# A fused two-layer attention block: VectorE normalises the second half of an attention result before it rounds the last quarter of the MLP's inner values

## What is computed

```
# layer 0
ln = layernorm(x);            x = x + attention(q(ln), k(ln), v(ln), causal) @ w_ao + b_ao     # stage A
ln = layernorm(x);            x = x + attention(q(ln), k(ctx), v(ctx), cross) @ w_co + b_co    # stage B
ln = layernorm(x);            x = x + gelu(ln @ w1 + b1) @ w2 + b2                             # stage M
# layer 1
a = layernorm(ctx);           x = x + tanh(gate) * attention(x @ Wq, a @ Wk, a @ Wv) @ Wo      # stage C
attention(q, k, v, mask):  softmax(q k^T / 4, masked) @ v, head by head
```

## Time and profile before

| | |
|---|---|
| median of 3 runs | 923.7 us (922.93 to 926.79) |
| the profiled execution: its time / its span | 922.3 us / 920.5 us |
| granted TensorE clock, mean | 0.970 of full speed (all of it in the full rounds looked at below) |
| PE busy | 855.6 us, 93% |
| VectorE (DVE) busy | 667.3 us, 72% |
| ScalarE (ACT) busy | 575.1 us, 62% |
| GpSimd (POOL) busy | 558.3 us, 61% |

### The profile page before, as it was taken

The page is one execution under the profiler, slowest core; times in us unless marked ns, Lnnn a source line. Parts: engine busy times, 40 slices in busy tenths (PEclk is TensorE's granted clock), DMA queues, the critical chain, the costliest instruction groups (busy, mean ns, idle before and its releaser), DMA issues.

```text
span 920.5 us, 24416 instructions
## 1 busy us (share of the span) xinstructions
PE 855.6 (93%) x9808; PEld 814.9 (89%) x9808; DVE 667.3 (72%) x1474; ACT 575.1 (62%) x1083; POOL 558.3 (61%) x565
## 2 busy tenths in 40 slices
PE   6687999999999999999999999999999999999895
PEld 5577988999999999999999999999999999998894
DVE  5737557878777787868787787868777786876553
ACT  6443556758484765758485765858486675848443
POOL 1436383938576592948667492948658493946341
PEclk9677899999999999999999999999999999999998
DMA  9000000010101010010101010010101000010000
GB/s 292 1 27 16 25 20 13 18 36 4 43 13 43 14 43 13 1 44 14 43 13 43 13 43 14 2 43 13 43 13 44 13 24 20 2 44 2 25 13 12
DMA packets 34142, 26.75 MB, mean 29 GB/s; under 512 B 12784, under 2 KB 33392, under 8 KB 34032
## 3 DMA queue, kind: packets, MB, share of 16 engines
q1 hardware_dynamic: 34032, 25.20, 9.4%
HBM read 20.99 MB, written 4.19 MB: 27 GB/s over the span
## 4 chain that ended last, share of the span: by engine, by line
PE 49%; DVE 17%; ACT 15%; POOL 11%; issue 7%; DMA 0%; DVEq 0%; SPq 0%; ACTq 0%; POOLq 0%
PE pj L475 11%; PE s_bank L539 7%; PE s_bank L514 6%; PE s_bank L525 6%; PE pj L489 5%; PE pj L456 5%; POOL prob_AC L1833 4%; PE pj L434 4%; ACT k L936 3%; ACT prob_AC L944 3%; ACT g L965 2%; DVE rmax_C L1292 2%; DVE h_hi L1798 2%; PE pj L552 2%; ACT L965 2%
## 5 line engine op out<-in xcount | busy, mean ns | idle before, releaser
L1813 POOL TENSOR_TENSOR rstd<-var_eps,half 128x2 f32<-128x2 f32 x64 | 48.9, 764 | 223.9 <-DVE var_eps L1338 223.9
L1833 POOL TENSOR_TENSOR prob_AC<-prob_AC,rmax_C 128x512 f32<-128x512 f32 x64 | 68.2, 1069 | 81.8 <-DVE rmax_C L1292 81.7
L944 ACT ACTIVATE prob_AC<-s_bank 128x512 f32<-128x512 f32 x128 | 72.0, 607 | 67.9 <-PE s_bank L525 67.7
L936 ACT ACTIVATE k<-pj,kbias,consts 128x256 f32<-128x256 f32 x192 | 92.6, 565 | 30.2 <-PE pj L456 27.7
L514 PE MATMUL s_bank<-k,q 64*128 64x128 f32 x1536 | 100.9, 282 | 8.3 <-ACT q L923 5.4
L514 PEld LDWEIGHTS s_bank<-k,q 64*128 64x128 f32 x1536 | 91.2, 190 | 16.3 <-ACT q L923 6.0
L1827 POOL TENSOR_TENSOR prob_B<-prob_B,maskB_off 128x512 f32<-128x512 f32 x64 | 81.5, 1284 | 13.7 <-DVE prob_B L1287 13.5
L1827 POOL TENSOR_TENSOR prob_AC<-prob_AC,maskA_off 128x512 f32<-128x512 f32 x64 | 81.3, 1280 | 12.2 <-DVE prob_AC L1287 12.2
L1840 POOL TENSOR_TENSOR h_lo<-g,h_hi 128x512 fp32r<-128x512 f32 x64 | 82.2, 1295 | 3.4 <-DVE h_hi L1798 3.4
L525 PE MATMUL s_bank<-consts,prob_AC 128*128 128x128 f32 x512 | 71.1, 281 | 11.2 <-POOL prob_AC L1833 8.6
L489 PE MATMUL pj<-w_hi_M,h_hi 128*128 128x256 f32 x256 | 76.1, 297 | 0.0
(11 more groups left out here) (207 smaller groups left out, 2938.0 us busy)
## 6 DMA issues: line engine op xcount, KB each, us to landing
x_in<-in_x SPq DMA_DIRECT2D x16, 256.0 KB, 2.6
ctx_b<-in_ctx_features SPq DMA_DIRECT2D x16, 256.0 KB, 3.3
ctx_c<-in_ctx SPq DMA_DIRECT2D x16, 256.0 KB, 3.0
out<-y SPq DMA_DIRECT2D x16, 256.0 KB, 2.2
maskB<-in_mask_Bx1xSxS_ff SPq DMA_DIRECT2D x32, 64.0 KB, 2.6
g<-in_w_M SPq DMA_DIRECT2D x2, 512.0 KB, 6.8
prob_AC<-in_w_A_qkv SPq DMA_DIRECT2D x3, 256.0 KB, 3.9
prob_B<-in_w_B_kv SPq DMA_DIRECT2D x2, 256.0 KB, 5.0
```

The costliest lines, as they stand in the source:

```text
L936: last = nc.scalar.activation(k2[:, m, :, s, :], k_all[:, m], ACT.Identity, bias=kbias[:, "ABC".index(a), s, m:m + 1], scale=parity[:, 2 + ...
L944: nc.scalar.activation(prob[a][:, r, :, :].rearrange("p n k -> p (n k)"), s_bank[r][:, :], ACT.Exp).then_inc(turned_in[a], 1)
L1813: nc.gpsimd.tensor_tensor(rstd[:, n, :], var_eps[:, n, :], half[:, :], ALU.pow).then_inc(ln_rstd[l], 1)
L1833: nc.gpsimd.tensor_tensor(p3, p3, rmax[a][:, r, :].unsqueeze(2).broadcast_to([P, BL * TILE, S]), ALU.subtract).then_inc(shifted[a], 1)
```

## The change

In DVE's `steady(i)`, `normalise("C", 1, i)` moves ahead of `high_h(3, i)`, to stand directly behind `normalise("C", 0, i)`. Nothing is added or removed, and no other engine's list changes. The fill and drain rounds have lists of their own and stay.

```
                 if active("C", i):
                     normalise("C", 0, i)
+                    normalise("C", 1, i)
                 if active("M", i):
                     high_h(3, i)
-                if active("C", i):
-                    normalise("C", 1, i)
                 if active("B", i):
                     row_max("B", 2, i)
```

## The result

| | before | changed |
|---|---|---|
| median | 923.58 us (7 runs, 922.93 to 926.79) | 917.77 us (7 runs, 913.68 to 919.48) |
| ratio, 95% interval | | 0.9927 [0.9903, 0.9950] |
| the profiled execution: its time / its span | 922.3 / 920.5 us | 917.77 / 916.0 us |

The change makes the kernel 5.8 us faster by the medians, where 8.8 was forecast. The interval leaves 1 out, and 917.8 lies between the 910.0 and 920.0 that were stated. The means are 917.10 and 923.89 us, 6.8 us apart; the ratio in the table is theirs (the medians alone would give 0.9937).

A forecast was written before the change was run, and what follows sets the result against it. PE, busy 93% of the span, was taken as the bound, with 1.09 us a round lost waiting for o_C. 12 x 0.7 + 0.38 = 8.8 us off 923.7 gave 914.9 us, range 910.0 to 920.0.

The forecast's parts named there:

- Step 1: Second half of o_C on DVE: done at 433.38, 0.7 before PE wants it; PE's wait of 1.09 us goes entirely.
- The test for being wrong from the start: PE's wait for the second half of o_C: if it stays in the changed profile, the prediction is wrong.
- Step 2: Cast of quarter 3 on DVE: about 1.15 us, starting at o_C's end, ending 0.29 behind low_h; its delay costs nothing.
- The lost turn: Rival: POOL's shift("B", 1) goes before the waiting cast, which ends at 435.50; 924.5 us, or 936 if twice; chance 0.06.
- The row given against the lost turn: The cast of 430.24 on DVE, said to ask in mid-instruction and come in before POOL's next one.
- Steps 3 and 4: DVE's row_max("B", 2) starts 0.62 us earlier; POOL's idle 0.40 before shift("B", 2) closes, its list ending 0.39 earlier.
- POOL is held by the cast for longer: Rival: shift("B", 1) ends at 435.54, POOL gains 0.25, PE 0.54 a round; 916.8 us; chance 0.07.
- Step 5: PE's next late input: POOL's shift("A", 3) at turn_probs("A", 3) limits the gain to about 0.7 us a round.
- the release of 0.06 us: Time from o_C done on DVE to PE's start, also used for POOL's shift("A", 3), leaving 0.29 of slack.
- The masks at `turn_probs("B", 1)`: PE's wait for DVE's second mask_scores("A"): 0.34 slack plus DVE's 0.62, a gain of at most 0.96 us.
- Step 6: The thirteenth round: bracket of 0.23 plus 0.15 of the last matmul's tail, a gain of 0.38 us.

The follow-up runs named there:

- e3: The change plus, on POOL, the residual sum of B moved behind shift A 3, against the kernel before: 913.25 us, ratio 0.9883.
- e7: The kernel before with only POOL's residual sum of B moved behind shift A 3, VectorE's order untouched: 919.49 us, ratio 0.9942.
- e9: The change plus row_max("B", 2) ahead of the cast high_h(3) on VectorE, run again for a profile, against the kernel before: 915.26 us, ratio 0.9917.
- e4: The change plus, on VectorE, the first two score masks of A ahead of row maximum B 3, against the kernel before: 914.30 us, ratio 0.9894.
- e1: The change itself run once more, against the kernel before: 918.16 us, ratio 0.9927.
- e5: The change plus POOL's residual sum of B behind shift A 3 and A's first two masks ahead of row maximum B 3: 915.01 us, ratio 0.9887.
- e8: The change in rounds 10 to 16 only, rounds 4 to 9 in the order before, against the kernel before: 922.18 us, ratio 0.9962.

## Why the prediction was right, and what was off

- Step 1, right. `o_C` of the second half is done 0.29 + 0.42 after its reciprocal starts, 0.68 ahead of PE's need (433.13 against 433.81), and PE's wait of 1.09 went entirely. The test for being wrong from the start did not occur. The sign named for it, `o_C` "some 0.6 us behind the first", does not fit the sum's own times: 433.38 is 0.91 behind 432.47, and 0.93 was measured.
- Step 2, right. The cast starts at 433.06 and ends at 434.24, 0.29 behind `low_h` (433.95), and takes 1.18 where about 1.15 was foretold. The lost turn occurred in no profile: in before, the change, e3, e7 and e9 the cast ends 0.27 to 0.29 after the POOL instruction that it met, and POOL's next one comes behind it. The row given against the lost turn was weak, though: POOL's next instruction behind the cast of 430.24 is the small `rstd`, beside which a cast took only 0.42 us (the rows at 422.81, under e7). The Trainium skill, page "SBUF — State Buffer", section "Who interferes with whom", says that of VectorE and GpSimd, whoever comes second at the shared pair of ports "**fully blocks**". For the cast the trace agrees, with e7's 0.40 passed on undiminished.
- Steps 3 and 4, right. The row maximum starts 26.42 us into the round instead of 435.04 - 408.01 = 27.03, 0.61 earlier, and `shift("A", 3)` ends at 448.60 - 407.74 = 40.86 instead of 41.26: 0.40 earlier, 0.39 foretold. That POOL is held by the cast for longer can be put aside: the two shifts take 2.23, as 1.23 + 1.04 less the overlap did. The Trainium skill's "until DVE-end + ~115 ns" (page "SBUF — State Buffer", section "A bandwidth-pool intuition that's wrong (but worth ruling out)"), a figure of descriptor generation, does not hold for these shifts: 434.24 + 0.115 + 2.04 for two free shifts would be 436.40, and they ended at 436.14.
- Step 5, the bound right and its size off. `turn_probs("A", 3)` decides, as forecast; e3 and e4 show it. The term that failed is the release of 0.06 us, taken from a wait of PE for DVE and used for a wait for POOL. Here POOL's shift ends at 448.60 and the transpose starts at 448.74: 0.14; in e4 it is 0.14 again (445.56 and 445.70). The room was therefore 0.21 + 0.40 = 0.61, not 0.68 to 0.72. Another 0.04 went behind it: from the last bank's transposes to the values it is now 0.56 us, and was 450.14 - 449.62 = 0.52. That leaves 0.57, seen as 0.56 on average, so that a round takes 51.65 and not 51.5.
- The masks at `turn_probs("B", 1)`, given as a bound of 0.96, do hold PE for 0.15; e4 shows that this costs nothing as long as POOL comes later.
- Step 6: 51.96 us became 51.54, 0.42 where 0.38 was forecast.
- The sum by what was measured: 12 x 0.56 + 0.42 = 7.1 instead of 8.8, so 1.7 of the 3.0 us that are missing by the medians are this term. The other 1.3 are not in the steady rounds. The prediction took fill and drain as unchanged, and for their work that is so; but their length varies from run to run by more than this. An estimate: if each execution's middle was as long as that of its kernel's profile, all else took 169.0 to 174.8 us in the 36 executions of the kernel before beside the experiments, and 168.1 to 174.4 in the 13 of the change and e1. The medians of these are 171.1 and 172.5, the means 171.7 and 172.0. So 1.0 of the 1.3 is the choice of the median (by the means the change gains 6.8 us). Whether the change also makes long ends a little more frequent is open.

## What to carry to other kernels

When a wait of the bounding engine is removed, follow each later release to see which list has the least room: here three lists had 0.6, 0.96 and 1.05 us against a wait of 1.09, and giving room to the list with the least (e3) brought 0.97 of the 1.09. Take the time from a release to a start from the same pair of engines, and look for waits shorter than one instruction inside merged rows (1.37 for eight where 1.04 is normal). Compare the like rounds of two profiles before trusting the difference of their totals. And ask why the blocking instruction is slow: the cast needs 0.42 us and took 1.57, so either order, on VectorE or on POOL, could be the one to change.

## What the runs showed of the hardware that was not expected

The ends of this program are uneven from run to run, and its middle is not; in the last round this goes with TensorE's granted clock. Over the middle the clock read 1.00 in all ten profiles of the table, over the fill 0.84 to 0.86. Busy time and clock of the last round, by stretches: before (one row), and e3 (one row); the clock is the figure ahead of the DMA share, 0.83 and 0.70:

```profile
897.50:920.50 23.00, 12.76 (x144) 10.43 (x142) 8.57 (x16) 7.71 (x13) 4.08 (x4) 0.83 0.04 12
```

```profile
887.48:913.70 26.22, 14.91 (x144) 12.39 (x142) 8.57 (x16) 7.71 (x13) 4.09 (x4) 0.70 0.03 11
```

The work is the same 144 matmuls, and VectorE's and ScalarE's busy times agree to a hundredth; PE needs 2.2 us more for it and the round is 3.2 us longer. In both the level falls from 2.4 to 1.2 GHz at the 16 transposes of `prob_AC`, after PE has waited 1.35 us for the queries and 2.36 for the softmax of the only unit left: near 905.7 in before, as they begin, and near 898.2 in e3, among the last of them. Before is back at full speed near 909.1, for the 64 value matmuls, and falls again near 915.9. The kernel e3 stays at half speed to the end. Busy time and clock in e3 (half speed, with 2.65 us of PE work in 5), and the value matmuls in before and in e3:

```profile
902.00:907.00 5.00, 2.65 (x34) 2.11 (x32) 1.86 (x6) 0.84 (x2) 0.00 (x0) 0.50 0.00 0
```

```profile
909.54 2.06 PE L539 MATMUL s_bank<-vz_AC,prob_AC 128*64 128x34 f32 x64
```

```profile
899.90 3.64 PE L539 MATMUL s_bank<-vz_AC,prob_AC 128*64 128x34 f32 x64
```

These 64 matmuls alone make 1.6 of the 3.2 us. They split all ten profiles the same way: 2.06 to 2.23 us in the six whose last round took 23.0 or 23.1 us, 3.6 us in the four with 26.1 or 26.2, nothing between. Three of those four are the kernels with the residual sum moved (e3, e5, e7), but the fourth, e8, has it where before has it. No profiled kernel showed both lengths, so whether an edit elsewhere shifts the odds is not settled. The fill took 145.7 to 149.2 us, and differed by 3.5 us between two profiles of one kernel, the change and e1.
